# Grouped attention: order of VectorE's step, who scales the weights, negated maxima, and a shorter opening

## The reference, cut to what matters

```python
ln_out = _ln(hidden_states, ln_w, ln_b)
q = _fp8_linear_pertensor(ln_out, wq, wq_scale, q_in_scale).reshape(b, s, g, hpg, d)
q = _ln(q, qln_w, qln_b)                      # k and qx in the same way
v = _fp8_linear_pertensor(ln_out, wv, wv_scale, v_in_scale).reshape(b, s, g, d)
core = _gqa(q, k, v)
kvx = einsum('bsi,oi->bso', cond, w_kv_x); kx, vx = split(kvx); kx = _ln(kx, kxln_w, kxln_b)
xout = _gqa(qx, kx, vx)
cat = concatenate([core, xout]); catq = _div_clamp_fp8(cat, proj_smooth)
return einsum('bsi,oi->bso', catq, wproj) * (proj_in_scale * proj_w_scale)
# _gqa: scores = q k / sqrt(d); p = softmax(scores); p v
```

## Time and profile before

| what | us |
|---|---|
| median of 3 runs | 2110.52 (2108.07 to 2111.7) |
| the profiled execution's own time | 2108.4 |
| its span | 2106.6 |
| attention stage in it | about 197 to 1126 |
| busy in the span: PE | 2022.6 (96%) |
| DVE | 1481.3 (70%) |
| ACT | 1183.6 (56%) |
| POOL | 660.9 (31%) |

### The profile page before, as it was taken

The page is one execution under the profiler, slowest core; times in us unless marked ns, Lnnn a source line. Parts: engine busy times, 40 slices in busy tenths (PEclk is TensorE's granted clock), DMA queues, the critical chain, the costliest instruction groups (busy, mean ns, idle before and its releaser), DMA issues. The chain is left out here.

```text
span 2106.6 us, 31981 instructions
## 1 busy us (share of the span) xinstructions
PE 2022.6 (96%) x11352; PEld 1576.0 (75%) x11352; DVE 1481.3 (70%) x3345; ACT 1183.6 (56%) x3027; POOL 660.9 (31%) x635
## 2 busy tenths in 40 slices
PE   8999899999999999999998999999999999998998
PEld 5645778888888888888876886665666785666997
DVE  2397778878787878787666837676677667885555
ACT  2073677777777777777764444553544446773332
POOL 1300344444444344444430002323341101222442
PEclk9999999999999999999999999999999999999999
DMA  4033433332424242332332203323322220002300
GB/s 182 22 118 109 142 108 114 95 120 86 144 73 142 84 135 79 116 102 81 105 99 80 96 1 146 117 85 125 115 105 112 85 71 22 2 2 101 125 1 32
DMA packets 60176, 193.71 MB, mean 92 GB/s; under 512 B 9409, under 2 KB 28641, under 8 KB 56049
## 3 DMA queue, kind: packets, MB, share of 16 engines
q1 hardware_dynamic: 48498, 172.16, 24.4%
q10 hardware_dynamic: 9504, 8.50, 1.4%
q0 software_dynamic: 2016, 11.01, 1.3%
HBM read 171.75 MB, written 19.49 MB: 91 GB/s over the span
## 5 line engine op out<-in xcount | busy, mean ns | idle before, releaser
L977 PE MATMUL psum<-la_w_both,context 128*128 128x256 f32 (+1 forms) x1536 | 343.6, 380 | 0.0
L977 PEld LDWEIGHTS psum<-la_w_both,context 128*128 128x128 f32 (+1 forms) x1536 | 277.3, 184 | 44.9
L1440 POOL TENSOR_TENSOR norm_std<-room 128x400 f32<-128x400 f32 x74 | 66.8, 902 | 251.7 <-DVE room L1203 251.7
L936 PE MATMUL psum<-qa_xqf,qa_two 128*128 128x400 f32 x640 | 142.2, 365 | 2.9 <-DVE qa_mv L1379 2.9
L936 PEld LDWEIGHTS psum<-qa_xqf,qa_two 128*128 128x128 f32 x640 | 119.2, 190 | 8.1 <-DVE qa_mv L1379 3.8
L3011 ACT ACTIVATE it_prob<-psum,it_nm 100x257 f32<-100x257 f32 (+1 forms) x256 | 101.7, 412 | 40.3 <-DVE it_nm L3042 40.2
L1127 ACT ACTIVATE qa_prob<-psum,qa_nm 100x361 f32<-100x361 f32 x128 | 71.8, 561 | 77.5 <-DVE qa_nm L1303 77.5
L1464 POOL TENSOR_TENSOR qa_yt<-qa_yb,qa_ym 128x400 f32<-128x400 bf16 x64 | 60.2, 941 | 164.8 <-DVE qa_ym L1336 164.8
L995 PE MATMUL psum<-qa_kxT,room 128*100 128x361 f32 x256 | 100.4, 474 | 10.9 <-DVE la_w_kt L1326 9.6
L1433 POOL TENSOR_TENSOR room<-room,qa_inv 128x500 f32<-128x500 f32 x64 | 83.3, 1302 | 62.0 <-DMA qa_inv<-qa_std_rows 53.6
L1300 DVE TENSOR_REDUCE qa_mx<-psum 100x2 f32<-100x722 f32 x64 | 58.2, 910 | 54.2 <-PE psum L996 54.1
(11 more groups left out here) (399 smaller groups left out, 5297.0 us busy)
## 6 DMA issues: line engine op xcount, KB each, us to landing
context<-in_context SPq DMA_DIRECT2D x70, 722.0 KB, 5.1
qa_inv<-qa_std_rows SPq DMA_DIRECT2D x64, 250.0 KB, 3.9
qa_w_raw<-in_qa_w SPq DMA_DIRECT2D x8, 1536.0 KB, 16.6
la_gf_raw<-in_gf_w SPq DMA_DIRECT2D x16, 768.0 KB, 4.7
qa_piece<-in_tf_pieces ACTq DMA_DIRECT2D x64, 128.0 KB, 2.0
la_w_qt<-in_qa_o SPq DMA_DIRECT2D x8, 1024.0 KB, 5.0
gf_ternary<-la_gf_made POOLq DMA_DIRECT2D x7, 768.0 KB
gf_ternary<-keep POOLq DMA_DIRECT2D x7, 768.0 KB
```

The lines of the kernel that those rows point to most:

```text
L936: mm = pe.matmul(psum[:, bank, 0:HALF], two[:, part, j, k, :], xqf[:, PART_XQ[j], k, (h % 2) * HALF:(h % 2 + 1) * HALF], start=(k == 0 and ...
L977: mm = pe.matmul(psum[0:rows, i // 2, (i % 2) * 256:(i % 2) * 256 + 256], ctxT[:, n % 2, k, t0:t0 + rows], kv_raw[:, s, k, :], start=(k == ...
```

## The change

It does these things in `grouped_attention`:

- DVE's `quantise` is split: `read_out(n - 1)` reads the output bank at the end of step n, ahead of the weight sums; the rounding stays at the start of the next step.
- `center_weights` becomes `mean_of_weights` (sum and mean alone, on DVE); the scalings move to ACT's `high_weights`. The value part is made at b = 6 on ACT, DVE and POOL instead of at b = 0 and 1.
- The maxima are negated by the reduction; L1303 and its semaphore go. The scale of the scores goes into `head_scale` and into two shifts made once.
- In DVE's step the order at the end becomes `probs_out`, `normalise_keys`, `unit_out`; it was `unit_out`, `normalise_keys`, `probs_out`.
- `FIRST` has five units; the sixth is done in step 0 with the seventh. PE no longer waits for `scales` ahead of its first matmul but ahead of the first variance. `invert_rows(0)` moves from the opening to step 0.

```diff
         def step_of(u):
             h, j = half_and_part(u)
-            return 4 * h - 5 + min(j, 3)
+            return max(4 * h - 5 + min(j, 3), 0) if h else j - PARTS
...
-        FIRST_BANKS = (2, 4, 5, 6, 7, 2)
+        FIRST_BANKS = (2, 4, 5, 6, 7, 6)
...
+        def ahead(n):
+
+            return units_of(n)[:-1] if n else []
+
+        def behind(n):
+
+            return units_of(n)[-1:] if n else units_of(n)
...
         def part_made(n, since):
 
             g, j = (n - since) // B, (n - since) % B
-            return (g + 1, j) if n >= since and j < PARTS and g + 1 < G else None
+            return (g + 1, j) if n >= since and j <= PARTS and g + 1 < G else None
...
PE:
                 project_values(g, s, b, n)
-                for u in units_of(n - 1):
+                for u in units_of(n - 1) if n else FIRST[-2:]:
                     variance(u)
...
+                if n == 1:
+                    pe.wait_ge(S_["raw_ready"], len(FIRST_BANKS))
...
-            pe.wait_ge(S_["scales"], 3)
             for u in FIRST:
                 project_unit(u)
                 if u >= 2:
                     variance(u - 2)
-            variance(FIRST[-2])
...
ACT:
             def high_weights(n):
...
-                act.wait_ge(S_["w_scaled"], (g - 1) * PARTS + j + 1)
-                act.wait_ge(S_["unit_mm"], PARTS * (2 * g - 1) + j + 1)
-                act.activation(two[:, 0, j], w_raw[:, :, PART_COL[j]:PART_COL[j] + P], ACT.Copy).then_inc(S_["w_hi"], 1)
-                if j == 0:
+                if j == PARTS:
+                    for k in range(C):
+                        last = act.activation(w_raw[:, k, V_COL:V_COL + P], w_raw[:, k, V_COL:V_COL + P], ACT.Copy,
+                                              scale=core.param("v_in", k))
+                    last.then_inc(S_["v_scaled"], 1)
                     act.wait_ge(S_["v_scaled"], g)
                     act.activation(v3[:, g % 2, 0], w_raw[:, :, V_COL:V_COL + P], ACT.Copy).then_inc(S_["v_hi"], 1)
+                    return
+                u, own = (g - 1) * PARTS + j, slice(PART_COL[j], PART_COL[j] + P)
+                act.wait_ge(S_["w_mean"], u + 1)
+                for k in range(C):
+                    last = act.activation(w_raw[:, k, own], w_raw[:, k, own], ACT.Identity, scale=core.param(PART_IN[j], k),
+                                          bias=w_mean[:, k:k + 1])
+                last.then_inc(S_["w_scaled"], 1)
+                act.wait_ge(S_["w_scaled"], u + 1)
+                act.wait_ge(S_["unit_mm"], PARTS * (2 * g - 1) + j + 1)
+                act.activation(two[:, 0, j], w_raw[:, :, own], ACT.Copy).then_inc(S_["w_hi"], 1)
...
-                    act.activation(prob[:, h, 0:TC], psum[0:T, 6 + h, 0:TC], ACT.Exp, scale=QK_SCALE,
+                    act.activation(prob[:, h, 0:TC], psum[0:T, 6 + h, 0:TC], ACT.Exp,
...
-                for u in units[-1:]:
+                for u in behind(n):
                     high_squares(u)
                 if not early(n, 1):
                     probs_out(n - 1)
...
DVE:
             def maxima(n):
                 dve.wait_ge(S_["s_mm"], n + 1)
-                dve.reduce_max(mx[:, 0:2], psum[0:T, 6:8, 0:TC], AX_X)
-                dve.reduce_max(mx[:, 2:4], psum[0:T, 6:8, TC:TC + T], AX_X).then_inc(S_["max_done"], 1)
-                dve.wait_ge(S_["max_done"], n + 1)
-                dve.tensor_scalar(nm[:, :], mx[:, :], -QK_SCALE, None, ALU.mult).then_inc(S_["nm_ready"], 1)
+                dve.reduce_max(nm[:, 0:2], psum[0:T, 6:8, 0:TC], AX_X, negate=True)
+                dve.reduce_max(nm[:, 2:4], psum[0:T, 6:8, TC:TC + T], AX_X, negate=True).then_inc(S_["nm_ready"], 1)
...
-            def quantise(g, s, b, n):
+            def read_out(g, s, b, n):
...
                 dve.wait_ge(S_["o_mm"], n + 1)
                 dve.tensor_tensor(yf[:, :, :], psum[:, 6, 0:4 * T].rearrange("p (j t) -> p j t", t=T),
                                   rsm[:, s, :].unsqueeze(2).broadcast_to([P, 4, T]), ALU.mult).then_inc(S_["o_read"], 1)
+
+            def quantise(n):
+
...
             def step(g, s, b, n):
-                units = units_of(n)
                 if not early(n, 2):
-                    quantise(*before(g, s, b, n, 2))
+                    quantise(n - 2)
                 values_out(b, n)
-                for u in units[:-1]:
+                if early(n, 1):
+                    invert_rows(0)
+                for u in ahead(n):
                     unit_out(u)
...
                 context_stats(n)
-                for u in units[-1:]:
-                    unit_out(u)
-                normalise_keys(n)
                 if not early(n, 1):
                     probs_out(n - 1)
+                normalise_keys(n)
+                for u in behind(n):
+                    unit_out(u)
...
                     add_out(quad, c, u)
-                center_weights(n)
+                if not early(n, 1):
+                    read_out(*before(g, s, b, n, 1))
+                mean_of_weights(n)
```

More of the change, by code:

```diff
@@ L846, in grouped_attention @@
         FIRST = [u for u in range(UNITS) if step_of(u) < 0]
-        FIRST_BANKS = (2, 4, 5, 6, 7, 2)
+        FIRST_BANKS = (2, 4, 5, 6, 7, 6)
         def bank_of(u):
-            return FIRST_BANKS[u] if u < len(FIRST) else 2
+            return FIRST_BANKS[u] if u < len(FIRST_BANKS) else 2
         def raw_of(u):
@@ L943, in variance @@
                 pe.wait_ge(S_["lo_ready"], u + 1)
+                if u == 0:
+                    pe.wait_ge(S_["scales"], 3)
                 if j == 0 and h:
@@ L1219, in invert_rows, with mean_of_weights @@
                 dve.reciprocal(own, own).then_inc(S_["inv_ready"], 1)
-            def center_weights(n):
+            def mean_of_weights(n):
                 made = part_made(n, 0)
-                if not made:
+                if not made or made[1] == PARTS:
                     return
@@ L1234, in center_weights @@
                                          ALU.mult).then_inc(S_["w_mean"], 1)
[L1235 to L1244, removed]
             def low_weights(n):
@@ L1260, in low_weights @@
                     dve.tensor_copy(v3[:, g % 2, 1], wv).then_inc(S_["v_mid"], 1)
+                    return
+                dve.wait_ge(S_["w_hi"], (g - 1) * PARTS + j + 1)
+                dve.tensor_tensor(two[:, 1, j], w_raw[:, :, PART_COL[j]:PART_COL[j] + P], two[:, 0, j],
+                                  ALU.subtract).then_inc(S_["w_lo"], 1)
             def split_o(g, c):
@@ L1381, in _ @@
             dve.tensor_tensor(row_scale[:, :], row_scale[:, :], row_scale[:, :], ALU.mult).then_inc(S_["scales"], 1)
-            for i, (one, other) in enumerate((("qln_w", "wq_scale"), ("kln_w", "wk_scale"), ("qxln_w", "wqx_scale"))):
-                dve.tensor_tensor(head_scale[:, i:i + 1], core.param(one), core.param(other), ALU.mult)
+            for i, (one, other, by) in enumerate((("qln_w", "wq_scale", QK_SCALE), ("kln_w", "wk_scale", 1.0),
+                                                  ("qxln_w", "wqx_scale", QK_SCALE))):
+                dve.scalar_tensor_tensor(head_scale[:, i:i + 1], core.param(one), by, core.param(other), ALU.mult, ALU.mult)
+            for i, name in enumerate(("qln_b", "qxln_b")):
+                dve.tensor_scalar(head_scale[:, 3 + i:4 + i], core.param(name), QK_SCALE, None, ALU.mult)
             dve.tensor_tensor(out_scale[:, :], core.param("proj_in_scale"), core.param("proj_w_scale"),
@@ L1405, in _ @@
             last = G * B - 1
-            quantise(G - 1, 1, B - 2, last - 1)
+            quantise(last - 1)
             maxima(last)
@@ L1413, in _ @@
             probs_out(last)
-            quantise(G - 1, 1, B - 1, last)
+            read_out(G - 1, 1, B - 1, last)
+            quantise(last)
             for i in range(2):
@@ L1448, in low_values @@
                 made = part_made(n, 1)
-                if made and made[1] == 0:
+                if made and made[1] == PARTS:
                     g = made[0]
```

22 lines of the change are left out of this document (9 added, 13 removed).

## The result

The changed kernel takes 2161.47 us in the median, the kernel before 2109.3 beside it: ratio 1.0241 (1.0225 to 1.0257), 52 us slower. One of the four executions was disturbed (2281.93 us at a granted clock of 0.93); it counts in this median and not in the ratio. The profiled execution took 2158.5 us, its span 2156.7, 50.1 us more than before.

What follows compares the result with a forecast made beforehand. TensorE was taken as the bound, busy 111.59 of 114.20 us a group. Terms +71.9 +5.8 +3.5 -18.3 -2.6 -0.8 = +59.5 us on the profiled 2108.4 gave 2167.9, as a median 2170.0 us; range 2150 to 2192.

Steps and rivals of the forecast that it cites:

- reordering: Weigh matmul, steps 1 to 58: ScalarE's copy waits behind squares that wait for unit_out; 1.24 us a step, +71.9 us.
- waiting for turned keys: Scores in half the steps wait 0.20 us more for ScalarE's turned keys; 29 steps, +5.8 us (0 to 12).
- scalings on ScalarE: Fourth step of a group: scalings ahead of ScalarE's exponentials make normalised weights late; 7 x 0.5 = +3.5 us.
- gains in the groups: Seven groups with weights to make: PE's whole standing time, 2.61 us each, goes; -18.3 us.
- behind step 58: Tail: exponentials start earlier as maxima are ready sooner; half of 5.2 us of waits credited, -2.6 us.
- opening: Sixth unit moved to step 0, wait for scales moved behind two units; gain of 0.8 us (loss 1.5 to gain 2.9).
- seven hand-overs: Engine-to-engine spacings in the reordering's chain from L1007's end to the weigh matmul; each 0.03 shorter would give 60 us.
- The step of my working that gave these gains to the earlier read: Output read ahead of the weight sums: the 9.6 us of L995 waits go; sums and rounding behind it cost nothing.
- the two stall terms: The weigh matmul's wait on ScalarE's copy, +71.9 us, and the scores' wait for turned keys, +5.8 us.
- nothing to spare: Step's end before the change: output projection L1030 just covers turning and copying the softmax weights ahead of weigh matmul L1014.
- Rivals 1 to 3: ScalarE's copy not held up, 2088.8 us (chance 0.07); ScalarE late throughout, 2201 (0.07); stall half as long, 2126 (0.06).

Runs made afterwards that it cites:

- b_reorder_alone: Kernel before with only VectorE's new order at the step's end (copies, key statistics, unit_out); 2161.86 us, ratio 1.0242.
- a_filler: Changed kernel plus eight idle matmuls ahead of the weigh matmul in steps 0 to 5, which have no output projection; 2147.0 us, ratio 1.0177.
- b_scale_on_act: Kernel before with only the weight scalings and the value part (at b = 6) moved to ScalarE; 2097.46 us, ratio 0.9942.

## Why the prediction was right

The time lies in the range, 8.5 us below the 2170.0 given; the mechanism, its place and its count (58) are as drawn. The sizes were less good, and errors of opposite sign cancelled. A plain step is 14.5 us and not 14.9, a group 120.1 and not 123. Term by term:

| term | forecast, us | in the traces, us |
|---|---|---|
| reordering | +71.9 | +58.0 |
| waiting for turned keys | +5.8 | +1.5 |
| scalings on ScalarE | +3.5 | +2.5 |
| gains in the groups | -18.3 | -15.6 |
| behind step 58 | -2.6 | -2.4 |
| opening | -0.8 | -1.7 |
| granted clock in steps 1 to 8, with what the opening lost in step 1 | 0 | +8.3 |
| rest | 0 | -0.2 |
| sum | +59.5 | +50.4, against 50.1 of span |

- *The reordering* was over-sized: 1.00 us a step, not 1.24. Two of the seven hand-overs were drawn too long: from the second copy to the next small operation it is 0.27 us and not 0.45 (that spacing was to an operation that waited for a matmul), and from ScalarE's copy to the weight load 0.04, not 0.11.
- *Waiting for turned keys* was over-sized, too: plain steps lose 0.05 us more than those with a second unit or two variances (1.05 against 1.00).
- *Scalings on ScalarE*: the fourth step grew by 1.35, that is 0.35 over the stall, not 0.5.
- *The gains in the groups* came in six groups, not seven. The second, fifth and sixth steps are as long as the first after the change, where they were 1.5, 0.4 and 0.7 longer; but in steps 2 to 8 of the kernel before, where the weights of the second group are made, there was no such excess. The step of my working that gave these gains to the earlier read fails: alone it costs 8 us, and ScalarE's scaling alone brings 12 and all of the 2.6 us a group. I costed sums and rounding behind the read at nothing, and beside that scaling they do cost nothing; with VectorE still scaling they don't hide.
- *Behind step 58* the number is met partly by luck: 0.7 of the 2.4 us comes with the new order, in b_reorder_alone as well, and I had put all of it down to the maxima and the read.
- *The opening* gave 1.3 us inside the stage (1.7 with what lay ahead of it), and lost it in step 1; the loss stands in the next term.
- *The clock* was no term at all: steps 1 to 8 lost 16.9 us, of which the stall and the small terms explain 8.6. The 8.3 us left (a_filler gives back 8.2) stand in for nearly half of what the two stall terms were over-sized by. The sum owes some of its closeness to that.

What I had taken for "nothing to spare" in the earlier trace rows was already a loss of 0.26 us in a plain step. Rivals 1 to 3 are out: the copy was held up, exponentials are late in one step of eight alone, and the stall is 1.0 and not 0.6. The rule of the Trainium skill that multiplies and adds belong on VectorE ("ScalarE: Activation LUTs", rules for kernel authors) gives speed per element as its reason. One scaling was faster on VectorE here as well: 0.28 us from start to start (1.12 for the four of L1237), against 0.41 on ScalarE. The conclusion isn't borne out by these runs: ScalarE had room, VectorE's queue had not, and the move is a gain (b_scale_on_act).

## What to carry to other kernels

When work on one engine is reordered, follow what each moved operation releases on the other engines, to the place where that wait stands in their queues. An operation that moved back behind two copies and two small operations moved back a whole chain here, because on ScalarE it stood in front of what TensorE wanted. The cheapest order for a late engine puts first what is ready first (`unit_out`, while PE still turns), then what the bound engine waits for, and what only a slack engine wants last. And parts don't add up: the early read cost 8 us by itself and nothing beside ScalarE's scaling, and copies that came earlier gained nothing in steps where PE then waited ahead of the scores. So parts are worth measuring alone and together, and a gain is worth tracing to the steps in which it should stand.

## What was not expected of the hardware

Added work that nothing needs made the changed kernel 14 us faster; some 8 us of that lie in steps 1 to 8, where it kept the granted clock at 1.00 instead of 0.90 over 75 us. A Vector operation of three elements per partition (L1295) took 0.83 us in the 58 steps in which it started just behind GpSimd's square, until that ended, and 0.22 us where GpSimd was quiet; an inverse of the same size beside the same square took 0.17. Moving the first behind the copies, together with that inverse, was worth 15 us of the whole time, about 12 of them in the loop.
